# Value blocks and early decoder products as sequences of their own, the dense part's squares on GpSimd, and all queues in a new order

## The reference

```python
x = x + attn0(xn) + moe(xn)            # layer 0
xn = layernorm(x)
x = x + sparse_attn(xn) + ffn(xn)      # layer 1
```

## Time and profile before

| what | value |
|---|---|
| median of 3 runs | 680.8 us |
| the profiled execution's own time | 682.07 us |
| its span (first to last instruction) | 680.3 us |
| TensorE busy | 642.2 us, 94% |
| VectorE busy | 550.7 us, 81% |
| ScalarE busy | 444.3 us, 65% |
| GpSimd busy | 367.6 us, 54% |
| chain that ended last | 70% TensorE, 18% VectorE, 5% ScalarE, 3% GpSimd |

### The profile page before, as it was taken

How to read it: one execution, slowest core, us unless ns; L and a number is a source line. 1 busy time by engine, 2 the same in 40 slices (tenths; PEclk the granted TensorE clock), 3 DMA queues, 4 the chain that set the end, 5 groups by cost and what they waited for, 6 DMA issues and landing times.

```text
span 680.3 us, 14252 instructions
## 1 busy us (share of the span) xinstructions
PE 642.2 (94%) x4792; PEld 435.5 (64%) x4792; DVE 550.7 (81%) x2461; ACT 444.3 (65%) x802; POOL 367.6 (54%) x448
## 2 busy tenths in 40 slices
PE   4888999999999999999999999999999999998785
PEld 3555765667556666766666567666657766675674
DVE  5998688746967999997986999984477999937996
ACT  3675454646687868557688877446879855478762
POOL 2288366646363688755463895665653577511220
PEclk9999899999999899999999999999999999999898
DMA  8930000000000000000000000000000000000000
GB/s 299 402 116 1 0 1 0 1 0 1 0 1 1 2 2 1 1 1 1 2 0 2 2 2 1 1 1 1 1 1 2 2 1 1 1 17 2 18 17 17
DMA packets 12968, 15.81 MB, mean 23 GB/s; under 512 B 1728, under 2 KB 10832, under 8 KB 12384
## 3 DMA queue, kind: packets, MB, share of 16 engines
q1 hardware_dynamic: 12896, 14.91, 6.3%
HBM read 13.85 MB, written 1.05 MB: 22 GB/s over the span
## 4 chain that ended last, share of the span: by engine, by line
PE 70%; DVE 18%; ACT 5%; POOL 3%; issue 3%; DMA 0%; DVEq 0%; POOLq 0%; ACTq 0%
PE bank_A L523 19%; PE bank_G L523 16%; PE bank_U L523 16%; PE bank_X L523 16%; DVE Wk L1269 4%; DVE m L1266 3%; DVE S L850 2%; DVE GWk L850 2%; PE bank_X L816 1%; PE bank_X L532 1%; ACT Ed L1336 1%; ACT L1341 1%; POOL PR L1643 1%; POOL Wlo L1643 1%; ACT L1336 1%
## 5 line engine op out<-in xcount | busy, mean ns | idle before, releaser
L1643 POOL TENSOR_TENSOR Wlo<-Wgu,Whi 128x256 fp32r<-128x256 f32 x184 | 136.2, 747 | 135.1 <-ACT Whi L1336 134.3
L523 PE MATMUL bank_A<-S,WdT 128*128 128x512 f32 x346 | 171.4, 598 | 0.2 <-POOL S L1643 0.2
L850 DVE TENSOR_TENSOR S<-S,bank_U 128x512 f32<-128x512 f32 x173 | 116.6, 682 | 35.1 <-PE bank_U L523 21.3
L1643 POOL TENSOR_TENSOR S<-S,Rb 128x512 f32<-128x512 f32 x84 | 109.3, 1302 | 56.4 <-DVE S L850 55.9
L523 PE MATMUL bank_G<-xH,Whi 128*128 128x512 f32 x184 | 99.6, 541 | 4.5 <-POOL Wlo L1643 2.3
L1336 ACT ACTIVATE Whi<-Wgu 128x256 fp32r<-128x256 f32 x184 | 73.4, 412 | 40.8 <-PE bank_U L523 36.1
L523 PE MATMUL bank_U<-xH,Whi 128*128 128x512 f32 x184 | 96.7, 525 | 0.1
L523 PEld LDWEIGHTS bank_A<-S,WdT 128*128 128x128 f32 x346 | 62.7, 190 | 33.9 <-issue 23.3
L1269 DVE MATCH_REPLACE8 Wk<-m,Wk 128x79 f32<-128x79 f32 x384 | 82.1, 225 | 0.0
L1336 ACT ACTIVATE S<-bank_G 128x512 f32<-128x512 f32 x90 | 53.6, 596 | 43.1 <-PE bank_G L523 37.9
L850 DVE TENSOR_TENSOR S<-Rb,bank_G 128x512 f32<-128x512 f32 x83 | 56.3, 679 | 25.6 <-ACT bank_G L1336 20.0
(11 more groups left out here) (294 smaller groups left out, 1184.9 us busy)
## 6 DMA issues: line engine op xcount, KB each, us to landing
Wgu<-in_Wgu SPq DMA_DIRECT2D x2, 2048.0 KB, 14.2
xs<-in_x SPq DMA_DIRECT2D x4, 256.0 KB, 6.0
wqk<-in_w_qkv SPq DMA_DIRECT2D x1, 1024.0 KB, 7.2
Wgu<-in_Wgu SPq DMA_DIRECT2D x1, 1024.0 KB, 8.9
out<-xs SPq DMA_DIRECT2D x3, 256.0 KB, 2.3
Wgu<-in_Wgu SPq DMA_DIRECT2D x1, 512.0 KB, 5.1
wout<-in_w_out SPq DMA_DIRECT2D x1, 512.0 KB, 7.7
wvT<-in_wvT SPq DMA_DIRECT2D x1, 512.0 KB, 8.5
```

The lines of the kernel that those rows point to most:

```text
L523: return engine.matmul(dst, lhsT, rhs, start=start, stop=stop)
L850: return engine.tensor_tensor(dst, a, b, op)
L1643: return engine.tensor_tensor(dst, a, b, op)
```

## The change

1. **Value blocks.** v0 and v1 leave the head's generator on TensorE and ScalarE and become `values` (letters k on PE, v on ACT), so that they can stand anywhere. In the banks they now come behind `pq`.
2. **Early decoder products.** For batch 3 the identity and `hq` products become `decode_early` (letter x on PE), which raises `dec_x`; the decoder step keeps the two `cc` products.
3. **Squares.** ScalarE makes only the relu of the dense part; GpSimd makes the square in place (`squares`, letter f), 16 of 128x512.
4. **Order.** All strings but SP's are new.

```diff
@@ uses()
-        for what in ("v0", "v1"):
-            add("U1" if last else "X2", what, b)
         for what in ("bdq", "hbm"):
             add("U0" if last else "X2", what, b)
-        add("U1" if last else "X2", "pq", b)
+        for what in ("pq", "v0", "v1"):
+            add("U1" if last else "X2", what, b)
@@ tensor_engine, head(b): the loop over v0, v1 leaves it
+            def values(b):
+                yTb = yT_of(b)
                 for k in range(2):
                     yield
                     t = fill(f"v{k}", b)
...
@@ decode(b, i), b == B - 1
-                t, c, h = fill("dec", b, i), cc[i % 2], slice(128 * i, 128 * i + 128)
-                pe.wait_ge("hq", 1)
...
-                mm(t[:, 0:128], ident, xb(b)[:, i, :], True, False)
+                t, c = ps("dec", b, i), cc[i % 2]
+                pe.wait_ge("dec_x", i + 1)
                 u = 2 * i + 1 + (i == NT - 1)
                 pe.wait_ge(empty(bank("ctx", b, u)), nth("ctx", b, u) + 1)
-                mm(t[:, 0:128], hq[:, h], dec[:, :], False, False)
                 mm(t[:, 0:128], c[:, 0, :], dec[:, :], False, False)
                 mm(t[:, 0:128], c[:, 1, :], dec[:, :], False, True).then_inc(sems(full(bank("dec", b, i))), 1)
+            def decode_early(b):
+                for i in range(NT):
+                    yield
+                    t = fill("dec", b, i)
+                    pe.wait_ge("hq", 1)
...
+                    mm(t[:, 0:128], ident, xb(b)[:, i, :], True, False)
+                    mm(t[:, 0:128], hq[:, 128 * i:128 * i + 128], dec[:, :], False, False).then_inc(sems("dec_x"), 1)
@@ scalar_engine, dense(b)
-                    a = emptied(act(r, t[:, :], ACT.Relu), "ff1", b, i)
-                    sc_.wait_ge(*a)
-                    act(r, r, ACT.Square).then_inc(sems("ffsq"), 1)
+                    emptied(act(r, t[:, :], ACT.Relu), "ff1", b, i)
@@ gpsimd_engine
+            def squares(b):
+                for i in range(NT):
+                    r = PR[:, 512 * (i % 2):512 * (i % 2) + 512]
+                    yield
+                    po.wait_ge(empty(bank("ff1", b, i)), nth("ff1", b, i) + 1)
+                    tt(r, r, r, ALU.mult).then_inc(sems("ffsq"), 1)
@@ ORDER["pool"], the first letters
-        "lyllllllalllmmmlaaacaclal...
+        "cclllyllllllammllaaaalmal...
```

More of the change, by code:

```diff
@@ L44 @@
     "pe":
[L45 to L49, removed]
@@ new lines @@
+        "mmeeeeeeeemmmeemmeemmeyeemseemesememeeemeeeemesemsmeeeeemmeemeeemeeeeemyeeymeeyeemeehmmeeeemmemmemee"
+        "meehemhemeeemeheeehhemymmeehhamheeeeeadkdeaeeedemmmmmaeeedaedemkateeeatdmedemtmetememeemdeeeemteteee"
+        "tmmemmeetemteemememeatmeeeeateateetmmteemeeeeemmeemtemeeatmmseeseeeheemsmtesemeyteymemteeeyehmetheee"
+        "mheemmhheeemmmmeeeheehmeemeheeeeykedmadeadeaeeamdaemdkatmaeeedeetemmmmeemdmtmeetmeeeeeedeemaemaeeeam"
+        "tmememeaeteeeemsmeeetseemmsteetmsmeemeetmeeememeeeetmemetemathmatmeeteaetamheehteaeeetmaetaemememmht"
@@ L76 @@
+        "mlmlllmlllmqmllfqlflmlmlqllpmlqmllmllqlmllmqmplllmlllqmmpmqfpfhfhfhffqqfqfqffqfffqfqq",
 }
@@ L768, in head @@
                 p.then_inc(sems(full(bank("pq", b))), 1)
+            def values(b):
+                yTb = yT_of(b)
+                for k in range(2):
+                    yield
+                    t = fill(f"v{k}", b)
+                    pe.wait_ge(empty(bank("y", b)), nth("y", b) + 1)
+                    for i in range(NG // 2):
+                        at = 64 * (NG // 2 * k + i) - 64
+                        o = slice(128 * i, 128 * i + 128)
+                        if at < 0:
+                            mm(t[0:64, o], yTb[:, 0:1].to_broadcast([128, 64]), encv[:, :])
+                            mm(t[64:128, o], yTb[:, 0:64], encv[:, :])
+                        else:
+                            p = mm(t[:, o], yTb[:, at:at + 128], encv[:, :])
+                    p.then_inc(sems(full(bank(f"v{k}", b))), 1)
             def distances(b):
@@ L840, in tensor_engine @@
             weave("pe", e=experts(), m=downs(), y=routes(), s=spreads(), u=setup(), a=attends(), f=every(dense_up), v=every(dense_down),
-                  h=heads(), d=every(distances), t=every(turns))
+                  h=heads(), k=every(values), d=every(distances), t=every(turns), x=decode_early(B - 1))
         def vector_engine(engine):
@@ L1523, in head @@
                 act(ksq[:, :], kp[:, PADK:], ACT.Square).then_inc(sems("ksq"), 1)
-                for k in range(2):
-                    yield
-                    t = filled(f"v{k}", b)
-                    if b > 0:
-                        q = NG // 2 * k + NG // 2 - 1
-                        sc_.wait_ge(full(bank("ctx", b - 1, q)), nth("ctx", b - 1, q) + 1)
-                    emptied(act(V[:, NG // 2 * k:NG // 2 * k + NG // 2, :],
-                                t[:, :].rearrange("p (g c) -> p g c", g=NG // 2), ACT.Relu), f"v{k}", b)
                 yield
@@ L1564, in head, with values @@
                     ACT.Copy).then_inc(sems("pk"), 1)
+            def values(b):
+                for k in range(2):
+                    yield
+                    t = filled(f"v{k}", b)
+                    if b > 0:
+                        q = NG // 2 * k + NG // 2 - 1
+                        sc_.wait_ge(full(bank("ctx", b - 1, q)), nth("ctx", b - 1, q) + 1)
+                    emptied(act(V[:, NG // 2 * k:NG // 2 * k + NG // 2, :],
+                                t[:, :].rearrange("p (g c) -> p g c", g=NG // 2), ACT.Relu), f"v{k}", b)
             def operands(b):
@@ L1634, in scalar_engine @@
             weave("act", x=highs(), e=silus(), m=sums(), y=every(route), s=every(spreads), c=scales(), u=setup(),
-                  a=every(attend), f=every(dense), h=every(head), o=every(operands), k=every(keys), n=every(near), g=every(gather), q=ends())
+                  a=every(attend), f=every(dense), h=every(head), v=every(values), o=every(operands), k=every(keys), n=every(near), g=every(gather), q=ends())
         def gpsimd_engine(engine):
@@ L1768, in every @@
                     yield from part(b)
-            weave("pool", c=zeros(), l=splits(), m=tiles(), y=every(route), a=every(attend), h=every(head), q=every(weights), p=adds())
+            weave("pool", c=zeros(), l=splits(), m=tiles(), y=every(route), a=every(attend), h=every(head), q=every(weights), p=adds(), f=every(squares))
         block = ctx.enter_context(nc.Block())
```

65 lines of the change are left out of this document (26 added, 39 removed).

## The result

The changed kernel takes 683.3 us (median of 11 runs, 682.2 to 689.1), the kernel before on the same chip 681.1 (11 runs): ratio 1.0053, 95% interval [1.0038, 1.0068]. It is slower; forecast was 677.2, and 683.3 lies above the range. Its profiled execution took 686.27 us for a span of 684.5, so the trace shows about 3 us more than the median.

The account below looks back on a forecast made before the run. Time was set by when TensorE saturates, the chain before the chooser, and what follows its last group. Front +0.2, chain -3.3, end -0.5 gave -3.6 us on the median 680.8: 677.2, range 673.2 to 681.2.

Parts of the forecast that it names:

- Together -4.1: Front up to 595.6 us: TensorE wait time regained by the new order, -4.1 us, with +0.5 for a new wait.
- The waits that it named: TensorE's waits before 595.6 us: 1.60 for `GWk`, 1.38 for a low weight half, 1.00 for `xn`, 1.6 for `mo`.
- prediction's own signs of being wrong: First matmul on time, TensorE's idle time from 17 to 200 us grown, or VectorE gaps between groups 3 and 8.
- The four half tiles in front of `rw`: Front, batch 0: g5, u5, u4, g6 on TensorE bring 2.8 us of work forward, against `rw` late by +3.8 +2.0.
- The start: GpSimd's clears at its queue's head hold VectorE's scalar steps and `xn`: 2.3 to 3.9 us late, 3.8 taken.
- The pile-up of the earlier trace: At 36.97 us four `xn` beside three Wlo took 3.00 for 1.11, losing 1.9; used to size the late start.
- The slower rival: Front: VectorE and GpSimd in lock-step, late start passes through (+3.8), second pile-up (+1.9): 682.7 us; chance 0.05.
- The chain before the chooser: Behind the last down product: earlier logarithm -0.9, six steps moved behind `hb` -3.7, smaller additions; -3.3 us at the chooser's end.
- +0.7 for La and the blocked step: Before the first distances: dense products where TensorE waited for La, +0.4; a GpSimd square about when VectorE makes `nmx`, +0.3.
- +0.6 for the second group: Chooser's second group: ScalarE's work between first and second distances takes 6.6 against VectorE's 6.05 us per group, +0.6.
- The end: Last decoder's four products, 2.02 us together: `hq` moves in front of the wait, a quarter gained, -0.5 us.
- The squares: Rival: twelve GpSimd squares behind the last down product each hold VectorE up to 1.03, 689.6 us; chance 0.04.

Follow-up runs that it names:

- new9: Changed kernel with before's order from tile 8 to the last down product, and one dense relu behind the second group's exponentials: 680.51 us, ratio 0.9989.
- of_clears: Before's order up to the last down product, changed order behind, plus the two `Wm` clears at the head of GpSimd's queue: 679.23 us, ratio 0.9989.
- c_hi: Changed kernel with before's start: both `Wm` clears and ScalarE's high half of tile 2 put back: 682.99 us, ratio 1.0037.
- c_small: Changed kernel with GpSimd's weight steps of tiles 3 to 19 cut to 8 of 512 columns, output not the reference's: 682.63 us, ratio 1.0023.
- old_front: Changed kernel with before's orders up to the last down product and the changed orders behind it: 677.23 us, ratio 0.9952.
- sq_back: `of_gap` with the dense part's squares back on ScalarE behind each relu, none on GpSimd: 677.6 us, ratio 0.9956.
- of_gap: `old_front` with one dense relu of the last batch moved on ScalarE behind the second group's logarithm and exponentials: 676.39 us, ratio 0.9951.

## Why the prediction was wrong

- **The step that failed** is the front's "Together -4.1; for a new wait of the usual size among so many moved places I put +0.5 (none to 1.6, the largest above)". The waits that it named did go. In their place came 1.58, 2.24, 2.64, 1.60 and 1.84 and smaller ones: idle time beyond the start grew by 3.7, where I had -3.6. Of the prediction's own signs of being wrong one came: idle time from 17 to 200 us grew, to 10.4 from 9.4. Bounding a new wait by the largest old one was wrong: the old waits were what a tuned order had left over, and no measure of what an untried one makes. The four half tiles in front of `rw` are not what makes the longest one: `new9` has them and no wait near 69 us.
- **A term that was missing**, the clock: 3.1 us of busy time in the profiled execution, and by the estimate above about 2.8 in the medians, as much as the whole difference to the kernel before. Without it the forecast of 677.2 would still have been missed by some 3 us, through the idle time.
- **The start**: 2.5 late in the trace for 3.8 predicted; a size, not the failed step. The clears did as said (held steps end at 6.1 and 7.1); one more small step lost 0.5, and the four `xn` met two Wlo and lost 0.4, not 1.9. The pile-up of the earlier trace rows was the wrong row to size them by. It passes through in the old order (2.0 in `of_clears`); in the changed kernel that stays open (`c_hi`: 2.6 in the trace, 0.3 in the medians).
- **The slower rival** named the place: "VectorE, not TensorE, is the bound from 17 to 51 ... and a second pile-up as at 36.97". The pile-up came, at 40.9 (`c_small` shows it). But its point of decision, saturation 5.2 us late, and its price, 682.7, left out the 2.64, which held steps lengthened as well, and the clock. That 682.7 lies near the measured 683.3 is luck. Its 0.05 was too little: the prediction itself listed several displaced steps beside a VectorE that was 92% busy, and each could be late.
- **The chain before the chooser** had the right mechanism and nearly the right size: -0.9 (measured -0.93), -3.7 (-3.87; the value copies alone 3.1), +0.7 for La and the blocked step (+0.3), +0.6 for the second group (+0.7): -4.0 for -3.3 at the chooser's end. A square did get in: the key mask's step took 1.30 beside it, `nmx` before it was spared. The gain is 1.6 less in executions whose clock falls in the first 12 us of this stretch (last section).
- **The end**: -1.2 for -0.5. The granted clock was 0.51 from the chooser's end in the kernel before and 0.78 in the changed one, so the last four products took 0.68 for 1.06. That is 0.4 of the 0.7 that I hadn't counted, and it is the clock's, not the change's.
- **The squares** didn't block the chooser (MAX8 227 ns); what they gain is not shown. `old_front` stands 3.7 below before in the medians, for a forecast of -3.8 for the same part: the miss lies in the front. That the two agree so closely is partly luck: behind the last down product the changed kernel's trace gains 5.1, and the splice takes some of that back.

## What to carry over

Here a change behind the bottleneck's last instruction could be summed from rows; a new interleaving in front of it couldn't, since engines that came past one wait ran into the next chain: keep the order that works there and splice the new one in behind, and look at what the splice itself costs. When several queues are reordered at once, cut the new order into the old one at a few points and time the cuts, before looking for a cause. An experiment that removes a cause must remove it at the wait in question: look at which instructions stand beside it. A wait's price is not its length alone: look at the granted clock behind it, and compare kernels at a like clock.

## What the runs showed of the hardware

**A held VectorE step can lose to several GpSimd instructions in turn.** In the changed kernel a 64x256 step of 0.42 (before) took 3.78, VectorE and GpSimd in the timeline:

```profile
359.87 3.78 DVE L859 TENSOR_TENSOR La<-PQ,cst 64x256 fp32r<-64x256 f32 x1
...
357.72 2.34 POOL L1696 TENSOR_SCALAR xn<-wk,rsum 128x64 f32<-128x64 f32 x8
360.02 0.75 POOL L1652 TENSOR_TENSOR Wlo<-Wgu,Whi 128x256 fp32r<-128x256 f32 x1
360.71 1.30 POOL L1652 TENSOR_TENSOR S<-S,Rb 128x512 f32<-128x512 f32 x1
361.94 1.43 POOL L1652 TENSOR_TENSOR Wlo<-Wgu,Whi 128x256 fp32r<-128x256 f32 x2
```

It ended at 363.65, right behind the last of them (363.37), four boundaries between GpSimd's instructions having passed. The Trainium skill ("SBUF — State Buffer", Who interferes with whom) says that whichever starts first holds the ports for its whole instruction and the other is blocked until it ends; of what happens when the next one is ready it says nothing, and here the waiting engine lost each time. The three held `lnv` steps and the three held `GWk` above waited for one instruction each. Why this one got in nowhere stays open.

**Long single waits of TensorE often came with a fall of its clock, short ones never did.** In the traces of 16 kernels (all but `sq_back`) I set the single waits of 1.5 us and more, from 17 us to 10 us behind the last down product, beside the granted clock. It counts as fallen when it went to the lower level during the wait or within 2 us of its end:

| wait | how many | clock fell |
|---|---|---|
| 2.2 to 2.9 us | 11 | 9 |
| 1.9 us (for `mo`, behind the last down product) | 15 | 6 |
| 1.80 to 1.84 us | 7 | 4 |
| 1.5 to 1.75 us | 27 | 0 |

The price can be read from the waits for `mo`, which the changed tail has in each of its 15 traces (0.79 in the kernel before): the instructions behind it are the same. `of_gap`, where the clock fell:

```profile
602.40 0.98 PE L534 MATMUL bank_X<-cst,mo 128*128 128x128 f32 x4 [1.89 <-DVE mo L867]
...
602.50:606.00 3.50, 3.50 (x14) 2.94 (x15) 0.27 (x1) 1.20 (x2) 1.65 (x3) 0.51 0.02 5
```

From the last down product to the first MAX8 it is 24.5 us in the six traces where the clock fell, and 22.9 in the eight with the same order where it didn't. Traces with the first twenty tiles in before's order have none to two stretches at the lower level up to 590 us, those with the changed order there one to four; that of 68 to 75 us above cost up to half its length, 3.4 us. Why the clock fell behind the 2.64 of the changed kernel and not behind its 2.24 stays open, and so do the stretches at 73 and 227 us of the kernel before, which stand behind no long wait.
